# Beta added to the diagonal of the adjacency chunk, expert counts on GpSimd, one semaphore per payload buffer, and eight split chunks in place of seven

## What is computed

```
z     = layernorm(x)                                   # 4096 x 128
scale = 1 / (sum(adj, axis=1) + beta)
x     = x + scale[:, None] * (adj @ z + beta[:, None] * z) @ kernel + bias
z1    = layernorm(x)
logits = z1 @ Wr + br; the 2 best experts, gates = softmax over the two
out   = sum over the two of gate * (relu(z1 @ W1[e] + b1[e]) @ W2[e] + b2[e])
x     = x + out
```

## Time and profile before

| | |
|---|---|
| median of 3 runs | 421.05 us (419.92 to 421.44) |
| profiled execution, its own time | 419.54 us |
| its span | 417.7 us |
| PE busy | 353.5 us (85%) |
| DVE busy | 299.8 us (72%) |
| POOL busy | 233.2 us (56%) |
| ACT busy | 163.7 us (39%) |

### The profile page before, as it was taken

One profiled execution on the slowest core, in us unless ns is written; L12 is line 12 of the kernel. 1 busy time (PEld: TensorE's weight loads), 2 busy tenths in 40 slices (PEclk: granted clock), 3 DMA queues, 4 the chain that ended last, 5 costly groups with the idle time before them and its releaser, 6 DMA issues.

```text
span 417.7 us, 8267 instructions
## 1 busy us (share of the span) xinstructions
PE 353.5 (85%) x2029; PEld 283.0 (68%) x2029; DVE 299.8 (72%) x881; ACT 163.7 (39%) x260; POOL 233.2 (56%) x219
## 2 busy tenths in 40 slices
PE   5999999979989999999998727199999999999300
PEld 2445777867858768778686423199999999999200
DVE  4644989779798997988987347066777777777157
ACT  3445654754845738548454030011212111112153
POOL 3450003076583885858838654246777777777600
PEclk9799999999999999999999958689999999999855
DMA  8999998997968969879691110779999999996087
GB/s 295 367 424 362 395 424 313 420 427 286 398 239 357 359 230 421 326 264 374 236 399 42 40 40 30 211 215 290 300 306 303 310 292 289 300 291 215 27 335 269
DMA packets 45479, 119.25 MB, mean 286 GB/s; under 512 B 7689, under 2 KB 19614, under 8 KB 37266
## 3 DMA queue, kind: packets, MB, share of 16 engines
q1 hardware_dynamic: 27794, 95.88, 61.9%
q10 hardware_dynamic: 12672, 14.58, 11.7%
q0 software_dynamic: 4992, 8.54, 5.7%
HBM read 104.02 MB, written 16.78 MB: 289 GB/s over the span
## 4 chain that ended last, share of the span: by engine, by line
PE 35%; POOL 22%; DMA 18%; issue 11%; DVE 10%; ACT 3%; POOLq 1%; SPq 0%; ACTq 0%; DVEq 0%
POOL dispatched_rows L488 16%; DMA dispatched_rows<-payload,slot 10%; PE bank L956 8%; PE bank L883 7%; PE bank L966 4%; PE bank_pair L966 4%; DMA expert_answers<-adj_ring,ans 3%; DVE adj_low L668 3%; PE bank L950 2%; POOL diag L475 2%; PE bank_pair L963 2%; PE bank L963 2%; DVE x_sb L824 2%; POOL payload L481 2%; DMA adj_ring<-adj_t 2%
## 5 line engine op out<-in xcount | busy, mean ns | idle before, releaser
L668 DVE TENSOR_TENSOR adj_low<-adj_ring,adj_high 128x2048 fp32r<-128x2048 f32 x49 | 113.8, 2332 | 27.7 <-ACT adj_high L550 27.6
L550 ACT CAST adj_high<-adj_ring 128x2048 fp32r<-128x2048 f32 x49 | 93.3, 1907 | 67.4 <-PE bank L897 40.5
L488 POOL DMA_INDIRECT dispatched_rows<-payload,slot x64 | 95.3, 1489 | 36.9 <-issue 29.0
L507 POOL DMA_INDIRECT expert_answers<-adj_ring,ans x92 | 90.5, 983 | 41.0 <-ACT adj_ring L600 20.9
L893 PE MATMUL bank<-adj_high,z_hi 128*128 128x512 f32 x196 | 79.6, 406 | 0.0
L894 PE MATMUL bank<-adj_high,z_lo 128*128 128x512 f32 x196 | 76.6, 391 | 0.0
L803 DVE TENSOR_SCALAR adj_ring<-bank,adj_ring 128x128 f32<-128x128 f32 x184 | 56.0, 346 | 14.4 <-PE bank L956 11.9
L883 PE MATMUL bank<-adj_ring,z_sb 128*128 128x512 f32 x120 | 55.9, 619 | 3.2 <-DVE z_sb L654 3.2
L956 PE MATMUL bank<-xt_sb,adj_ring 128*128 128x128 f32 x368 | 57.1, 278 | 0.0
L897 PE MATMUL bank<-adj_low,z_hi 128*128 128x512 f32 x196 | 52.7, 390 | 0.0
L956 PEld LDWEIGHTS bank<-xt_sb,adj_ring 128*128 128x128 f32 x368 | 49.5, 195 | 0.0
(11 more groups left out here) (129 smaller groups left out, 430.5 us busy)
## 6 DMA issues: line engine op xcount, KB each, us to landing
adj_ring<-adj_t SPq DMA_DIRECT2D x64, 1024.0 KB, 8.9
adj_ring<-w_pack SPq DMA_DIRECT2D x48, 257.5 KB
adj_ring<-w_pack ACTq DMA_DIRECT2D x44, 257.5 KB
dispatched_rows<-pad_rows SPq DMA_DIRECT2D x8, 528.0 KB, 10.9
adj_ring<-expert_answers SPq DMA_DIRECT2D x8, 512.0 KB, 7.0
adj_ring<-dispatched_rows SPq DMA_DIRECT2D x48, 66.0 KB
adj_ring<-dispatched_rows ACTq DMA_DIRECT2D x44, 66.0 KB
out<-x_sb SPq DMA_DIRECT2D x8, 256.0 KB, 4.3
```

The lines of the kernel that those rows point to most:

```text
L488: pool.indirect_dma_start(rows, bass.IndirectOffsetOnAxis(ap=slot[:, b, i:i + 1], axis=0), payload[:, b, t, k, :], None).then_inc(scattere ...
L507: pool.indirect_dma_start(y_tok, bass.IndirectOffsetOnAxis(ap=ans[:, s:s + 1], axis=0), y_sb[:, s, :], None, bounds_check=N * K - 1, oob_i ...
L550: nc.scalar.copy(high[:, m % PARTS], adj_sb[:, slot_of(g, k)]).then_inc(hi_ready, 1)
L668: v.tensor_tensor(low[:, m % PARTS], adj_sb[:, slot_of(g, k)], high[:, m % PARTS].bitcast(F32), ALU.subtract).then_inc(lo_ready, 1)
```

## The change

1. The product with `diag` goes, with `own_product`, `zi` and `agg_done`. In its place POOL adds the diagonal of beta to the four 128x128 blocks of the chunk that holds the group's own rows (`add_diag`, one instruction for three blocks and one for the fourth, after the one that makes `diag`), in the ring buffer. PE's or ACT's use of that chunk waits for `diag_added`. The chunks of a group are taken in another order (`chunk_order`), so that this one comes at position 6, in group 7 at position 7; the batches of z follow that order, and there are six of them.
2. All eight chunks of a group are split (SPLIT = 8). ACT rounds and DVE subtracts one more chunk per group, z_hi and z_lo cover all 32 tiles.
3. The count `more` and the running `seen` are made by POOL: two additions for `more`, one for `seen`, in `dispatch`. The mask of the next group and `ranks` wait for `seen_ready`.
4. Each payload buffer has a semaphore for its scatters. POOL doesn't wait for them any more; `normalise` waits for those of two groups before.
5. `chosen` goes (the index is used directly), the difference of the two best logits is one instruction at the end, `ranks` stands before tile 27, and the low parts of the next group all follow `place`.

```diff
-SPLIT = 7
+SPLIT = 8
-BATCHES = ((0, 4), (4, 4), (8, 8), (16, 8), (24, 8))
-X_BEFORE = (1, 3, 4, 5)
+BATCHES = ((4, 4), (8, 4), (12, 8), (20, 8), (0, 4), (28, 4))
+X_BEFORE = (1, 3, 4, 6)
+DIAG_AT = [CHUNKS - 2] * (GROUPS - 1) + [CHUNKS - 1]
...
+def chunk_order(g):
+
+    if g == GROUPS - 1:
+        return list(range(CHUNKS))
+    others = [k for k in range(CHUNKS - 1) if k != g]
+    return others + [g, CHUNKS - 1]
...
+            def add_diag(g):
+                k = DIAG_AT[g]
+                own.after(pool.tensor_tensor(diag[:], ident[:, None, :].to_broadcast([P, GT, P]),
+                                             beta_sb[:, group(g)].to_broadcast([P, GT, P]), ALU.mult))
+                pool.wait_ge(adj_in[slot_of(g, k)], landed(g, k))
+                chunk = adj_sb[:, slot_of(g, k)].rearrange("p u n -> p (u n)")
+                most = (CJ - 1) * (GN + P)
+                blocks = chunk[:, 0:most].rearrange("p (u n) -> p u n", u=CJ - 1)[:, :, 0:P]
+                pool.tensor_tensor(blocks, blocks, diag[:, 0:CJ - 1, :], ALU.add)
+                own.after(pool.tensor_tensor(chunk[:, most:most + P], chunk[:, most:most + P], diag[:, CJ - 1, :], ALU.add))
+                pool.sem_inc(diag_added, 1)
...
             def dispatch(g):
                 b = g % 2
                 pool.wait_ge(z1_ready, g + 1)
                 pool.tensor_copy(payload[:, b, :, 1, 0:D], payload[:, b, :, 0, 0:D])
                 own.after(pool.tensor_copy(payload[:, b, :, :, ANSWER], answer_tab[:, group(g), :]))
-                pool.wait_ge(prefilled, 16 * PAD_DMAS)
+                pool.wait_ge(mask_ready, g + 1)
+                own.after(pool.tensor_tensor(more[:], mask[:, 0:2, :], mask[:, 2:4, :], ALU.add))
+                own.after(pool.tensor_tensor(more[:, 0, :], more[:, 0, :], more[:, 1, :], ALU.add))
+                pool.wait_ge(rank_done, g + 1)
+                pool.tensor_tensor(seen[:], seen[:], more[:, 0, :], ALU.add).then_inc(seen_ready, 1)
+                if g == 0:
+                    add_diag(2)
+                    pool.wait_ge(prefilled, 16 * PAD_DMAS)
                 pool.wait_ge(slots_ready, g + 1)
                 for t in range(GT):
+                    if t == 2 and 0 < g < GROUPS - 3:
+                        add_diag(g + 2)
                     for k in range(K):
...
-                pool.wait_ge(scattered, (g + 1) * (GT * K * 16))
-                pool.sem_inc(payload_free, 1)
+                if g == GROUPS - 3:
+                    add_diag(GROUPS - 1)
...
             def round_chunk(g, k):
...
+                if k == DIAG_AT[g]:
+                    act.wait_ge(diag_added, g + 1)
...
             def copy_agg(g):
-                act.wait_ge(agg_done, g + 1)
+                act.wait_ge(chunk_used, (g + 1) * CHUNKS)
...
             def normalise(g):
                 act.wait_ge(shift_ready, g + 1)
                 if g >= 2:
-                    act.wait_ge(payload_free, g - 1)
+                    act.wait_ge(scattered[g % 2], all_scattered(g - 2))
...
                 round_chunk(g, 6)
+                round_chunk(g, 7)
                 for k in range(PARTS):
                     round_chunk(g + 1, k)
...
                 choose(g - 1)
-                low_part(g + 1, 0)
+                low_part(g, 7)
                 place(g - 1)
-                low_part(g + 1, 1)
-                low_part(g + 1, 2)
+                for k in range(PARTS):
+                    low_part(g + 1, k)
...
             def gnn(g):
                 if g > 0:
-                    pe.wait_ge(seen_ready, g)
+                    pe.wait_ge(var1, g)
...
             def ranks(g):
                 pe.wait_ge(mask_ready, g + 1)
+                if g > 0:
+                    pe.wait_ge(seen_ready, g)
...
-                    if j == 26:
+                    if j == 27:
                         ranks(g - 1)
```

More of the change, by code:

```diff
@@ L59, in batch_of, with half_made @@
 def batch_of(j):
-    return max(b for b, (first, _) in enumerate(BATCHES) if first <= j)
+    return next(b for b, (first, count) in enumerate(BATCHES) if first <= j < first + count)
+def half_made(b):
+    return sum(count // 2 for _, count in BATCHES[:b])
 def dve_half(b):
@@ L408, in _ @@
                 load_weights(sp, starts[s], s)
[L409 removed]
+            for b in range(2):
+                sp.wait_ge(scattered[b], all_scattered(GROUPS - 2 + b))
             for s in range(SP_SLOTS):
@@ L460, in _, with low_z @@
             pool.sem_inc(consts, 1)
[L462 to L468, removed]
-            pool.wait_ge(params_in, 16 * 5)
[L471 to L476, removed]
+            def low_z(b):
+                tiles = high_tiles(b)
+                if not tiles:
+                    return
+                pool.wait_ge(z_hi_ready, b + 1)
+                for first in range(tiles[0], tiles[-1] + 1, GT):
+                    quad = slice(first, first + GT)
+                    pool.tensor_tensor(z_lo[:, quad, :], z_sb[:, quad, :], z_hi[:, quad, :].bitcast(F32),
+                                       ALU.subtract).then_inc(z_lo_ready, 1)
+            def add_diag(g):
[9 more added lines that the diff above has]
+                pool.sem_inc(diag_added, 1)
+            pool.wait_ge(params_in, 16 * 5)
+            for b in range(len(BATCHES)):
+                low_z(b)
+            add_diag(0)
+            add_diag(1)
             def dispatch(g):
@@ L529, in high_z @@
             def high_z(b):
[L530 to L534, removed]
+                tiles = high_tiles(b)
+                if not tiles:
+                    return
+                act.wait_ge(z_by_act, half_made(b + 1))
+                act.wait_ge(z_by_dve, half_made(b + 1))
+                nc.scalar.copy(z_hi[:, tiles[0]:tiles[-1] + 1, :], z_sb[:, tiles[0]:tiles[-1] + 1, :]).then_inc(z_hi_ready, 1)
             root_z(0)
@@ L717, in place @@
                 own.after(last)
-                own.after(v.tensor_reduce(rank[:], work[:].rearrange("p t k e -> p (t k) e"), AX_X, ALU.add))
-                v.scalar_tensor_tensor(out=slot[:, g % 2], in0=chosen[:].rearrange("p t k -> p (t k)"), scalar=float(EXPERT_ROWS),
+                own.after(v.tensor_reduce(rank[:], work[:], AX_X, ALU.add))
+                v.scalar_tensor_tensor(out=slot[:, g % 2], in0=top_i[:, :, 0:K], scalar=float(EXPERT_ROWS),
                                        in1=rank[:], op0=ALU.mult, op1=ALU.add).then_inc(slots_ready, 1)
@@ L743, in _ @@
             place(GROUPS - 1)
+            v.tensor_tensor(diff[:], top[:, :, 1], top[:, :, 0], ALU.subtract).then_inc(diff_ready, 1)
             dve.wait_ge(total_done, 1)
```

89 lines of the change are left out of this document (38 added, 51 removed).

## The result

The changed kernel takes 429.59 us (median of 4 runs, 428.94 to 432.33), the kernel before 420.49 beside it; the ratio is 1.0245 [1.017, 1.032]. It is 2.4% slower: outside the predicted range, on the side that had a chance of 0.24. The profiled execution took 429.8, its span 428.0 us (before 417.7), 10.3 more.

The account below looks back on a forecast made before the run. DVE was taken to bound a group at 27.35 us. Choose of group 3 at 119.3, four groups and 7.5 put the aggregate's end at 236.2 (before 236.37); -0.6 us in all gave 418.9, or 420.4 by medians; range 414 to 425.

Parts of the forecast that it names:

- the side that had a chance of 0.24: Whole kernel: the outcome slower than before; the forecast gave faster 0.34 and same 0.42.
- That is where DVE begins choose of group 3: Group 3: DVE starts choose at 119.3 us, after POOL's late addition, a rounding, a low part and one collision.
- POOL's chain: POOL from pads landed through dispatches 0 and 1: start 84.5, addition for group 3 done at 114.2 us.
- about 5.8 us: Group 3: DVE's stall, once, since DVE alone would have begun choose at 113.5 instead of 119.3 us.
- Thereafter POOL has some 22 us of work in 27 and is early: Groups behind group 3: POOL has about 22 us of work in a 27 us group, so no further stall.
- the fourth rival: Every group: addition waits for the chunk to land; landings 1 us later give 28.4 us groups, 424.6 us total; chance 0.10.
- PE waiting 1.65 us for the copy: Each group's end: PE waits about 1.65 us for ACT's aggregate copy, which stands behind a rounding of 1.90 us.
- My sum for PE (26.6): Each group: PE alone needs 26.6 us, 24.97 of work plus about 1.65 waiting for the aggregate's copy.
- my 27.0: Quiet group: DVE's loop with the eighth low part, without collisions, takes 27.0 us and sets the group's pace.
- where I took 0.35: Each group: DVE loses 0.35 us to port collisions with POOL, making a group 27.35 us, bounds 27.0 and 28.5.
- The third rival: Every group: collisions with POOL set DVE's pace, 1.15 us more a group, so 28.5; 425.0 us total; chance 0.14.
- PE's saving void: Each group: what PE sheds, 0.71 us by the eighth split chunk and 0.81 by the product, DVE takes up.

Follow-up runs that it names:

- addition_early: Changed kernel with POOL's addition for group 3 moved, within dispatch 1, from behind four scatters to before the first; 426.78 us, ratio 1.019 to the kernel before.
- all_but_group3_attached: Changed kernel with the addition of group 3 alone sent to a scratch tile, nothing waiting for it; 429.94 us, ratio 1.0273 to the kernel before.
- the six kernels named above: Six follow-up kernels, each an edit of the changed kernel, that share a DVE stall of 3.34 to 3.36 us in group 1.
- seven_split: Changed kernel with seven split chunks instead of eight and the earlier order of low parts; 428.56 us, ratio 1.0202 to the kernel before.
- semaphores_alone: Kernel before the change plus only a scatter semaphore per payload buffer, so POOL no longer waits for its scatters; 419.36 us, ratio 0.9952.
- additions_unattached: Changed kernel with POOL's additions made on a scratch tile and no rounding or PE waiting for them; 417.78 us, ratio 0.9935 to the kernel before.
- product_back: Changed kernel with beta added by PE's product with diag again, not on the chunk; 419.74 us, ratio 0.9997 to the kernel before.
- product_back_seven: product_back with seven split chunks and the earlier order of low parts; 413.6 us, ratio 0.9824 to the kernel before the change.
- after: The changed kernel itself, with the whole change; 429.59 us, ratio 1.0245 to the kernel before.
- only_group3_attached: additions_unattached, but in group 3 POOL adds into the chunk and the rounding waits for it; 426.73 us, ratio 1.0185 to the kernel before.
- clock_bridged: Changed kernel with useless PE products filling its waits before the first gnn and before ranks of groups 1 and 2; 426.02 us, ratio 1.0149.
- eight_split_alone: Kernel before the change with all eight chunks split and DVE's new order of low parts, nothing else; 424.48 us, ratio 1.0126.
- counts_on_dve: Changed kernel with the count and seen made by DVE again; 429.56 us, ratio 1.0215 to the kernel before.

## Why the prediction was wrong

The step that failed is the term of the sum "That is where DVE begins choose of group 3", 119.3; it came at 124.51, 5.2 us of the 10.5 by which the end (236.2 foreseen, 246.7) is off. The others: group 4 30.3 and not 27.35 (+2.95), the two quiet groups +1.5, the last +0.35, and from the last choose to the end 8.0 and not 7.5. What the runs showed in its place: the rounding of group 3 was released at 120.24 and not at 114.2, groups 1 and 2 were late before it, and the group behind it ran on a slower clock.

**POOL's chain, right in kind, 6.0 us short.** I had the addition of group 3 done at 114.2, it was at 120.24. 3.45 of it is the start (84.5 foreseen, 87.95). The chunk to which addition 2 is made landed at 83.44; with 1.35 us the addition would have been done at 84.8, near enough. It took 3.5 us, 2.51 of it for an instruction that takes 0.46 alone, and another 1.02 passed before the first scatter. Then the eight scatters took 15.4 (17.1 foreseen), the preparation 4.2 (2.8; a copy of 2.60 beside a low part), four scatters 10.1 (7.4), diag and additions 2.6 (2.4). From there to choose it took 4.3 and not 5.1, so 6.0 becomes 5.2. I had an upper bound of 3.5 for the addition and chose 1.35; POOL's instructions in front of a deadline should have been summed at the prices that they have beside a low part. The wait itself I had at "about 5.8 us", and DVE's is 5.50: the mechanism was right, its arrival not, since group 2 was late by itself as well.

**A single stall: wrong.** "Thereafter POOL has some 22 us of work in 27 and is early" holds for quiet groups only. `addition_early` and `all_but_group3_attached` show group 4 paying when group 3 doesn't. And the queue is one half only. In group 2, and in group 1 of the six kernels named above, POOL was idle until the chunk had landed, and the addition was late because landing and addition together left no room. That is the mechanism of the fourth rival, in the groups where I hadn't looked for it: in quiet groups, of which it spoke, the addition ends 1.3 us before the rounding wants it (177.45 and 178.79 in group 5), and of the kernels with the addition at position 6 only `seven_split`, with a chunk less to round, waits there.

**PE's clock: not in the prediction.** I had PE waiting 1.65 us for the copy (it waits 1.72) and counted that as idle time only. In group 1, where the wait is 2.67, the clock fell to 0.54, and about 1.6 us of the group's delay of 2.7 at its choose (61.46 against 58.79 in the earlier trace rows) is that: from gnn to the next chunk PE takes 4.39 us, before 2.82. This part isn't shown to come from the change, for the profiled run of `semaphores_alone`, which has the product, has it too (wait 2.25, then 0.51 in 43.8 to 47.2, choose at 61.68). In quiet groups the product with diag, 0.81 us of PE's time that I booked as saved, stood in this gap: with it back PE waits 0.81, without it 1.72. My sum for PE (26.6) held both numbers and was right; what I didn't say is that they are the same time, so that taking the product away gives PE nothing.

**DVE's loop: right in its base, collisions mis-sized.** Without collisions the quiet group is about 26.7, near my 27.0. With them it is 28.1: the mask takes 0.71 (0.42 without), one low part 2.86 (2.28) and shift 0.77 (0.16), together 1.5 where I took 0.35. The third rival came near for a quiet group (28.5 there). By its own sum a group of 27.5 us is already level with before (119.3 + 4 x 27.5 + 7.5 - 0.4 = 236.4), not one of 27.9. The Trainium skill, "SBUF — State Buffer", section "SBUF: two separate sides", calls this pair's port a lock held for the whole instruction; the row that shows it here is shift, 128x4 elements, which takes 0.77 us for 0.16. But collisions are not what made the kernel slow: `additions_unattached` has them too and is the faster one.

**The counts, the semaphores, group 0.** The counts on POOL are worth nothing measurable alone (0.9824 against 0.9886, intervals overlap). The semaphore per buffer gives 0.5% (0.9952 [0.9915, 0.9988]), where I had said nothing by itself. The copy of group 0's aggregate starts 1.1 us later (42.91 against 41.81), behind a rounding that waited 2.29 us for its chunk to land, but so it does in `semaphores_alone` (43.11), where nothing is added to a chunk; the addition of group 0 was in time.

**The eighth chunk.** I called PE's saving void because DVE takes it up. It is worse: the group gets 1.2 to 1.3 us longer (27.9 against 26.6), since without it PE would have set a shorter pace; `product_back` against `product_back_seven`, 1.7% apart.

Open: how the 10.3 us split between stalls and clock in groups 1 and 2. Group 1's own stall differs from kernel to kernel (0.57 us in the profiled run of after, 3.34 to 3.36 in six of the others); the first addition took 1.22 us there and 2.5 to 2.8 in the six, and the runs without a profile don't show it. `only_group3_attached` against `additions_unattached` is 6.5 us in the profiled runs and 10 by the ratios, so one profile may not be typical. Nor is it shown that the clock alone accounts for 3.6 us, since the filling products also move what follows: the quiet groups of `clock_bridged` take 27.8 us and not 28.1.

## What to carry to other kernels

An in-place edit by a helper engine ahead of the first step of the critical chain puts the helper's whole queue on that chain. Sum that queue from its first real start (here pads and a chunk landing), each instruction at the price it has beside the busy engine, and do it for every group until the helper is a group ahead, not for the one group that looks tightest. An idle helper can be late too: landing plus the edit at its dear price has to fit before the step that waits.

Before booking the removal of a short product as a gain, look at what its engine does in the same moment: if it waits right after, the time isn't saved, and a longer wait can be followed by a slow stretch that costs more than the product.

When two engines are both nearly full, moving load between them only helps toward the one that has room, so try the parts singly: here the best version keeps the semaphores, the small savings of choose and the later `ranks`, and drops the addition and the eighth split chunk; where the counts are made is all one.

## What the runs showed of the hardware

- Single waits of PE of 1.90 and 2.25 us (`semaphores_alone`, then 0.51 in 94.9 to 98.0 and in 43.8 to 47.2), 2.15 (`eight_split_alone`, 0.63), 2.67, 3.01 and 3.75 us (after) were followed by stretches near 1.2 GHz. Those of 2.25 (`product_back_seven`) and 2.57 us (`additions_unattached`), both in group 1, of 3.02 (`clock_bridged`, group 1) and 3.75 (`counts_on_dve`, group 3), and several of 1.62 to 1.72 were not. So the length of one wait does not decide it: 2.25 and 3.75 us stand on both sides. In `clock_bridged` the clock stayed at 1.00 in all groups.
- An indirect DMA issue takes POOL 0.96 us in DVE's pauses and 2.2 to 3.07 beside low parts; in after, a 128x128 addition 0.46 and 2.51, a 128x512 copy 0.61 and 2.60.
